# Raw scores and maxima nearer to the scores, their transposition in the raw bank at the beat's end

## The chip, the cores and the metric

The kernel runs on one core of a Trainium2 chip. The metric is the device time in microseconds (us) of one execution, as the median of several runs. The engines are TensorE (PE, with its weight loads shown apart as PEld), VectorE (DVE), ScalarE (ACT), GpSimd (POOL) and SyncE (SP), which only issues DMAs here.

## The reference

One transformer block with conditioning and a second residual, for 32 sequences of 128 tokens with 128 channels:

```
a = x + attention(norm1(x))          # 16 heads of 8 channels, softmax over 128 keys
y = a + swiglu(norm2(a))             # 512 hidden channels
out = x + y
norm(x) = gain(cond) * x * rsqrt(mean(x*x) + eps) + bias(cond)
attention: softmax(q k^T / sqrt(8)) v, then Wo;  swiglu: silu(x Wg) * (x Wh) Wo
```

All of it is in float32. The kernel splits float32 numbers into a high and a low part (or into three bfloat16 parts for queries and keys), so that products of the parts give the accuracy.

## The kernel before

The 32 sequences are cut into G = 8 groups of four. A group's attention takes eight beats, each with half the heads (four heads of either half) of one sequence. The main loop runs over beats T = 0 to 78; in each, every engine does what `due(T, offset, n, every)` says is due: a step with offset o of group g falls into beat 8g + o. All stages of different groups so run side by side in one hand-written order, the same in every beat, and every engine executes its list strictly in that order. Beat T computes the scores of T.

The softmax subtracts the row maximum inside the score product: two rows of the stacked queries hold the negated maximum as a high and a low bfloat16 part. So the maxima must be known before the scores. They are had in these steps:

- `b_raw(g, t)` on PE (L383): eight small products give raw scores into the PSUM buffer `raw` of two banks (in the prologue of group 0 also into `score`). It waits until the maximum of the raw scores before it has been taken.
- `b_max(g, t)` on DVE (L766): a reduction over `raw` gives the negated maxima of that beat, into `nmax`.
- `b_maxT(g, half)` on PE (L393): after four maxima, the half of `nmax` is transposed into the fourth quarter of the bank `pv`.
- `b_shift(g, half)` on DVE (L776, L778): copies it to bfloat16, then subtracts to get the low part.
- `shift_rows(g, half)` on SP (L262): four small DMAs, for each of two sequences one of the high and one of the low part, write the rows into the stacked queries `qs`.
- `c_score(g, t)` on PE (L410) waits for those rows in beats t = 0, 2, 4, 6 of the group.

In the kernel before, raw scores run seven beats ahead of the scores (RAW = -7), and the transpositions lie at offsets -3 and +1 (MAXT = -3, every 4), so in beats 5 and 1 mod 8, one beat after the fourth and eighth maximum. The prologue does the raw scores 0 to 6 of group 0 and the first transposition. `c_pv` of the beat after a transposition waits for the second shift instruction, since it writes the bank that this one reads.

PE's order in a beat: `c_score`, `b_raw`, `c_pv` (L427), `c_tro` (L442, transposition of o_s, odd beats), `d_gate_up` (L320 to L322, the two products into the hidden layer), `b_maxT`, `a_transpose` (L334, odd beats), `d_out` (L489), `c_wo` (L446, odd beats), `d_xt2` (L454, even beats), `c_tr2` (L437, even beats), values, keys and queries of a later group.

DVE's order: `d_final`, `c_x1` (L803, L806, even beats), `d_hi` (L814), the rests of queries and keys (L738), `b_max`, `b_shift`, `d_hidden` (L823 gated, L828 hT), `c_norm` (L786 reciprocal, L791 o_s, even beats), `a_hi` (L730). ScalarE's: `a_high`, the exponential (L607), `c_ot` (L613), the middle part of keys (L600), `c_oT` (L619), `d_tanh` (L636), mean squares (L569), `d_norm` (L625), `a_norm` (L577), the middle part of queries (L600), values (L588).

The gate_up product of a piece goes to the one bank `ffn` and waits for the hT of the piece before, until piece SPREAD; from there on it goes round `raw`'s two banks and `ffn`. SP's order in a beat is store (L268), `shift_rows`, stacking of queries and keys (L254).

Of the kernel before, what the change touches and what calls it, by code (L numbers as in the profile page):

```python
# [15 lines left out]
def bass_cond_transformer_block(  # L16
# [10 lines left out]
    L, B, D = x.shape  # L27
# [5 lines left out]
    G = B // NB  # L33
# [3 lines left out]
    HQ = 4  # L37
# [26 lines left out]
    MEAN, INV1, SCALE1, XT1, HI1 = -30, -28, -26, -23, -15  # L64
    VALUE, KEY, QUERY = -7, -14, -13
    STACK = -12
    RAW, MAXT = -7, -3
    PV = 1
    OT, TR2, NORM, TRO, WO, X1, INV2, XT2, HI2, RESID = 2, 2, 2, 3, 3, 4, 5, 6, 7, 6
    FFN, OUT, FINAL, WSTEP = 10, 15, 17, HC + 1  # L70
    LAST = BEATS * (G - 1) + FINAL + WSTEP
    SPREAD = BEATS * G + RAW + 1 - FFN

    ctx = ExitStack()
    with ctx:
# [146 lines left out]
            return (tok, ffn)[b % 2][:, 0:L] if early(g) else score[:, (b % 2) * 512:(b % 2) * 512 + L]  # L222

        def raw_dst(g, t):
            return score if g == 0 and t % 2 and t < BEATS - 1 else raw

        def key_dst(g):
            return pv if g == 1 else proj
# [88 lines left out]
        def _(pe):  # L317
# [50 lines left out]
            def b_raw(g, t):  # L368
                if t == 0:
                    pe.wait_ge(s_stack[buf(g)], stacked(g))  # L370
                if g == 0:
                    if t == 0:
                        pe.wait_ge(s_xn1, 2 * NB)
                    if t == BEATS - 1:
                        pe.wait_ge(s_max, t)
                    elif t >= 2:
                        pe.wait_ge(s_max, t - 1)
                else:
                    pe.wait_ge(s_max, BEATS * g + t)
                for j in range(HQ):  # L380
                    for e in range(HALVES):
                        h8 = HQ * (t % 2) + j
                        mm = pe.matmul(raw_dst(g, t)[:, pair_cols(e, j)],  # L383
                                       qs[buf(g)][tile_rows(e, RAW_ROWS), h8, batch_cols(t)],
                                       ks[buf(g)][tile_rows(e, RAW_ROWS), h8, batch_cols(t)], start=True, stop=True)
                mm.then_inc(s_raw, 1)

            def b_maxT(g, half):
                pe.wait_ge(s_max, BEATS * g + HQ * (half + 1))
                if g == 0 and half == 0:  # L390
                    pe.wait_ge(s_nmax0, 2)
                    pe.wait_ge(s_krest, 2)
                pe.transpose(pv[:, 3 * L:4 * L], nmax[g % 2][:, half * 128:half * 128 + 128],  # L393
                             ident[:]).then_inc(s_maxT, 1)

            def c_score(g, t):
                if t % 2 == 0:
                    pe.wait_ge(s_shiftrow[buf(g)][t // 2], shifted(g))
                if t == 0 and g < NBUF:
                    pe.wait_ge(s_onerows[g], 32)  # L400
                if g == 0 and t == 0:
                    pe.wait_ge(s_max, BEATS - 2)
                for f, b in due(BEATS * g + t - 1, XT1, NB, 2, since=3):
                    pe.wait_ge(s_xn1, NB * f + b + 1)
                if BEATS * g + t > 0:
                    pe.wait_ge(s_exp, BEATS * g + t)
                for j in range(HQ):
                    for e in range(HALVES):
                        h8 = HQ * (t % 2) + j
                        mm = pe.matmul(score[:, pair_cols(e, j)],  # L410
                                       ks[buf(g)][tile_rows(e, HALF_ROWS), h8, batch_cols(t)],
                                       qs[buf(g)][tile_rows(e, HALF_ROWS), h8, batch_cols(t)], start=True, stop=True)
                mm.then_inc(s_score, 1)

            def c_pv(g, t, T):
# [3 lines left out]

                for f, i in due(T - 1, XT2, NB, 2):  # L420
                    pe.wait_ge(s_xn2, NB * f + i + 1)
                for f, half in due(T - 1, MAXT, 2, HQ):
                    pe.wait_ge(s_slo, 2 * f + half + 1)
                for e in range(HALVES):
                    for j in range(HQ):
                        at = e * HH * VW + (HQ * (t % 2) + j) * VW
# [29 lines left out]
            def d_gate_up(g, p):  # L456
# [6 lines left out]
                if 0 < n < SPREAD:  # L463
                    pe.wait_ge(s_h, n)
                elif SPREAD <= n < SPREAD + 2:
                    pe.wait_ge(s_max, BEATS * G)
                elif n >= SPREAD + 2:
                    pe.wait_ge(s_h, n - 2)
                cs = slice(ch * 128, ch * 128 + 128)
# [51 lines left out]
            unread_products(4)  # L521
            b_raw(0, 4)
            b_maxT(0, 0)
            b_raw(0, 5)
            a_transpose(2, 0)
            a_transpose(2, 1)
            a_values(0)
            a_transpose(2, 2)
            b_raw(0, 6)
            a_transpose(2, 3)  # L530
            for T in range(LAST + 1):
                for g, t in due(T, 0, BEATS):
# [6 lines left out]
                    c_tro(g, i)  # L539
                for g, p in due(T, FFN, PIECES):  # L540
                    d_gate_up(g, p)
                for g, half in due(T, MAXT, 2, HQ):
                    b_maxT(g, half)
                for g, b in due(T, XT1, NB, 2, since=3):
                    a_transpose(g, b, T)
                for w in range(WIN):
# [3 lines left out]
                    c_wo(g, i)  # L550
                for g, i in due(T, XT2, NB, 2):
                    d_xt2(g, i, T)
                for g, i in due(T, TR2, NB, 2):
                    c_tr2(g, i)
                for g, _ in due(T, VALUE, since=1):
# [159 lines left out]
        def _(dve):  # L715
# [54 lines left out]
            def b_shift(g, half):  # L770

                dve.wait_ge(s_maxT, 2 * g + half + 1)
                if g > 0:
                    for b in range(MB):
                        dve.wait_ge(s_shiftrow[buf(g - 1)][MB * half + b], shifted(g - 1))
                dve.tensor_copy(shift[:, half, 0, :], pv[0:MROWS, 3 * L:4 * L]).then_inc(s_shi, 1)  # L776
                dve.wait_ge(s_shi, 2 * g + half + 1)
                dve.tensor_tensor(shift[:, half, 1, :], pv[0:MROWS, 3 * L:4 * L], shift[:, half, 0, :],  # L778
                                  ALU.subtract).then_inc(s_slo, 1)

            def c_norm(g, i):
# [83 lines left out]
            for t in range(HQ):  # L865
                b_max(0, t)
            b_shift(0, 0)
            for t in range(HQ, BEATS - 1):
                b_max(0, t)
            for T in range(LAST + 1):  # L870
                for g, w in due(T, FINAL, WIN, WSTEP):
                    d_final(g, w)
# [187 lines left out]
```

## Time and profile before

| | us |
|---|---|
| median of 3 runs | 257.99 |
| lowest, highest | 257.29, 258.37 |
| the profiled execution's own time | 255.85 |
| its span | 254.0 |
| first score, last exponential (start) | 32.39, 230.65 |

The share of the span in which each engine was busy, the busy time by tenths in 40 slices of 6.35 us, and the clock granted to TensorE:

```profile
span 254.0 us, 8307 instructions
...
PE   3496677779989999999989999999999999899894
PEld 2384454457668868786878877877787878687893
DVE  4648866888898989889888998899888997564673
ACT  5355748867865786569756776667757655666430
POOL 8324852695283345526282526152623232324310
PEclk9999979999999999999999999999999999999999
```

A digit 9 is 90% or more of a slice. The steady loop fills the slices from about the tenth to the thirty-fourth. A matmul's end is modelled, so that a busy PE is not PE at its peak. Times in the text without a unit are places in the trace, in us from the start of the span.

### The profile page before, as it was taken

The page shows a single profiled execution, that of the slowest core. Times are in us where ns is not written, and L with a number is a line of the kernel's source. Part 1 is how long each engine was busy: PE and PEld are TensorE (multiplying, and loading weights), DVE is VectorE, ACT ScalarE, POOL GpSimd, SP SyncE. Part 2 cuts the span into 40 slices and gives each one's busy share as a digit, 9 for nine tenths or more (in the row PEclk, how much of TensorE's full clock was granted, in tenths as well). Part 3 has the DMA queues.
Part 4 walks back from the last instruction along what each step waited for, and adds up shares of the span by engine and source line. Part 5 has one row for each costly group of instructions (what it writes and reads, how often), then busy time and mean ns, then how long its engine had stood idle before and what let it go on. Part 6 is the DMA issues. An engine that isn't in the chain of part 4 may idle for free.

```text
span 254.0 us, 8307 instructions
## 1 busy us (share of the span) xinstructions
PE 223.3 (88%) x3084; PEld 180.8 (71%) x3084; DVE 203.0 (80%) x490; ACT 163.4 (64%) x352; POOL 112.0 (44%) x183
## 2 busy tenths in 40 slices
PE   3496677779989999999989999999999999899894
PEld 2384454457668868786878877877787878687893
DVE  4648866888898989889888998899888997564673
ACT  5355748867865786569756776667757655666430
POOL 8324852695283345526282526152623232324310
PEclk9999979999999999999999999999999999999999
DMA  5867602510360026001530054004500000000001
GB/s 166 343 169 169 169 4 65 156 45 5 85 170 1 27 66 186 26 24 40 156 85 18 11 151 122 4 26 128 147 3 26 1 26 3 23 3 25 22 23 41
DMA packets 18819, 18.79 MB, mean 74 GB/s; under 512 B 3644, under 2 KB 17980, under 8 KB 18652
## 3 DMA queue, kind: packets, MB, share of 16 engines
q1 hardware_dynamic: 18252, 17.80, 24.9%
q10 hardware_dynamic: 528, 0.46, 0.8%
q8 instruction: 25, 0.41, 0.7%
q14 instruction: 14, 0.11, 0.2%
HBM read 3.22 MB, written 2.10 MB: 21 GB/s over the span
## 4 chain that ended last, share of the span: by engine, by line
PE 43%; issue 24%; POOL 16%; DVE 6%; ACT 4%; SPq 3%; ACTq 1%; DMA 1%; POOLq 0%; DVEq 0%
PE proj L489 7%; PE pv L427 6%; PE ffn L320 5%; PE score L410 4%; PE ffn L322 3%; PE ffn L321 3%; SPq L254 3%; POOL inv L933 3%; PE raw L383 2%; POOL qp L925 2%; PE tok L442 2%; POOL xn_lo L946 2%; POOL kp L925 2%; POOL xs L939 2%; POOL xn_lo L918 2%
## 5 line engine op out<-in xcount | busy, mean ns | idle before, releaser
L766 DVE TENSOR_REDUCE nmax<-raw 128x8 f32<-128x1024 f32 x61 | 74.2, 1217 | 2.8 <-PE raw L383 2.6
L607 ACT ACTIVATE p_s<-score 128x1024 f32<-128x1024 f32 x64 | 65.4, 1022 | 17.1 <-PE score L410 15.9
L427 PE MATMUL pv<-p_s,va 128*32 128x128 f32 x1024 | 41.7, 280 | 1.9 <-ACT xn L625 1.2
L320 PE MATMUL ffn<-xn_hi,ffn_hi 128*128 128x256 f32 x106 | 34.8, 328 | 1.2 <-POOL xn_lo L946 1.2
L636 ACT ACTIVATE th<-ffn 128x256 f32<-128x256 f32 x53 | 20.4, 384 | 19.6 <-PE ffn L322 19.6
L489 PE MATMUL proj<-ffn_out_s,hT 128*128 128x128 f32 x240 | 31.6, 275 | 0.0
L823 DVE SCALAR_TENSOR_TENSOR gated<-th,ffn 128x256 f32<-128x256 f32 x53 | 22.0, 415 | 12.0 <-ACT th L636 11.7
L427 PEld LDWEIGHTS pv<-p_s,va 128*32 128x32 f32 x1024 | 24.7, 109 | 9.3 <-issue 4.1
L946 POOL TENSOR_TENSOR xn_lo<-xn,xn_hi 128x128 fp32r<-128x128 f32 x32 | 14.7, 460 | 34.6 <-DVE xn_hi L814 34.6
L322 PE MATMUL ffn<-xn_hi,ffn_lo 128*128 128x256 f32 x106 | 29.7, 280 | 0.0
L321 PE MATMUL ffn<-xn_lo,ffn_hi 128*128 128x256 f32 x106 | 29.6, 279 | 0.0
L489 PEld LDWEIGHTS proj<-ffn_out_s,hT 128*128 128x128 f32 x240 | 29.2, 191 | 0.0
L410 PE MATMUL score<-qs,ks 64*128 64x128 bf16 x512 | 25.6, 220 | 2.6 <-ACT p_s L607 0.9
L933 POOL TENSOR_TENSOR inv<-ms,mhalf 128x1 f32<-128x1 f32 x32 | 17.4, 544 | 21.5 <-DVE ms L806 21.5
L320 PEld LDWEIGHTS ffn<-xn_hi,ffn_hi 128*128 128x128 f32 x106 | 21.4, 202 | 6.5 <-issue 4.2
L383 PE MATMUL raw<-ks,qs 62*128 62x128 bf16 x488 | 24.0, 217 | 1.4 <-DMA qs<-qp 0.9
L410 PEld LDWEIGHTS score<-qs,ks 64*128 64x128 bf16 x512 | 14.6, 94 | 14.6 <-issue 9.7
L828 DVE SCALAR_TENSOR_TENSOR hT<-gated,ffn 128x256 f32<-128x256 f32 x53 | 22.3, 421 | 1.8
L625 ACT ACTIVATE xn<-pv,mod 128x128 f32<-128x128 f32 x32 | 14.5, 454 | 10.0 <-PE pv L454 9.1
L321 PEld LDWEIGHTS ffn<-xn_lo,ffn_hi 128*128 128x128 f32 x106 | 20.1, 189 | 0.0
L322 PEld LDWEIGHTS ffn<-xn_hi,ffn_lo 128*128 128x128 f32 x106 | 19.9, 188 | 0.0
L925 POOL TENSOR_TENSOR qp<-q_rest,qp 128x512 bf16<-128x512 f32 x7 | 8.7, 1240 | 23.3 <-ACT qp L600 23.3
(132 smaller groups left out, 469.2 us busy)
## 6 DMA issues: line engine op xcount, KB each, us to landing
ks<-kp SPq DMA_DIRECT2D x48, 128.0 KB, 2.4
qs<-qp SPq DMA_DIRECT2D x45, 128.0 KB, 2.5
out_y<-x_s SPq DMA_DIRECT2D x16, 128.0 KB, 1.8
x_s<-in_x SPq DMA_DIRECT2D x1, 1536.0 KB, 10.0
qs<-shift SPq DMA_DIRECT2D x64, 4.0 KB
x_s<-in_x SPq DMA_DIRECT2D x2, 256.0 KB, 3.5
ffn_in_s<-in_ffn_in_w SPq DMA_DIRECT2D x1, 512.0 KB, 6.7
qs<-qp ACTq DMA_DIRECT2D x3, 128.0 KB, 3.7
```

The lines of the kernel that those rows point to most:

```text
L320: pe.matmul(dst, w_hi, v_hi, start=True, stop=False)
L321: pe.matmul(dst, w_hi, v_lo, start=False, stop=False)
L322: return pe.matmul(dst, w_lo, v_hi, start=False, stop=True)
L383: mm = pe.matmul(raw_dst(g, t)[:, pair_cols(e, j)], qs[buf(g)][tile_rows(e, RAW_ROWS), h8, batch_cols(t)], ks[buf(g)][tile_rows(e, RAW_ROW ...
L410: mm = pe.matmul(score[:, pair_cols(e, j)], ks[buf(g)][tile_rows(e, HALF_ROWS), h8, batch_cols(t)], qs[buf(g)][tile_rows(e, HALF_ROWS), h8 ...
L427: mm = pe.matmul(pv[VW * j:VW * j + VW, (t % 2) * L:(t % 2 + 1) * L], va[vbuf(g)][:, t // 2, at:at + VW], p_s[:, (BEATS * g + t) % PBUF, p ...
L489: mm = pe.matmul(out_dst(g, w)[:, b * D:(b + 1) * D], hT[:, HC * w + ch, b * L:(b + 1) * L], ffn_out_s[:, ch, :], start=(ch == 0 and b == ...
L607: act.activation(p_s[:, n % PBUF, :], score[:], ACT.Exp, scale=SCALE).then_inc(s_exp, 1)
L766: dve.tensor_reduce(heads[:, :, t % 2, :], raw_dst(g, t)[:].rearrange("l (e j m) -> l e j m", e=HALVES, j=HQ), AX.X, ALU.max, negate=True) ...
L823: dve.scalar_tensor_tensor(out=gated[:], in0=th[:, p % 2, :], scalar=1.0, in1=ffn_dst(n)[:, 0:PW], op0=ALU.add, op1=ALU.mult).then_inc(s_g ...
L828: dve.scalar_tensor_tensor(out=hT[:, p, :], in0=gated[:], scalar=0.5, in1=ffn_dst(n)[:, PW:2 * PW], op0=ALU.mult, op1=ALU.mult).then_inc(s ...
L933: pool.tensor_tensor(inv2[:, i:i + 1], ms2[:, i:i + 1], mhalf[:, 0:1], ALU.pow).then_inc(s_inv2, 1)
```

## The change

The raw scores and maxima run five beats ahead of the scores (RAW = -5), the transpositions lie at offsets -2 and +2 (beats 6 and 2 mod 8), in the beat of the fourth and eighth maximum itself. PE does them at the end of the beat, after `d_xt2` and before `c_tr2`, and they write the first quarter bank of `raw` (only the very first one still `pv`). The raw scores after a transposition (t = 0 and 4) wait for the second shift instruction; `c_pv` no longer does, except in the first beat. The prologue has two raw scores and two maxima fewer. DVE's, ScalarE's and SP's lists within a beat stay as they are. SPREAD goes from 48 to 53: pieces 48 to 52 stay on the one bank.

```diff
--- before.py
+++ after.py
@@ -64,12 +64,12 @@
     MEAN, INV1, SCALE1, XT1, HI1 = -30, -28, -26, -23, -15
     VALUE, KEY, QUERY = -7, -14, -13
     STACK = -12
-    RAW, MAXT = -7, -3
+    RAW, MAXT = -5, -2
     PV = 1
     OT, TR2, NORM, TRO, WO, X1, INV2, XT2, HI2, RESID = 2, 2, 2, 3, 3, 4, 5, 6, 7, 6
     FFN, OUT, FINAL, WSTEP = 10, 15, 17, HC + 1
     LAST = BEATS * (G - 1) + FINAL + WSTEP
-    SPREAD = BEATS * G + RAW + 1 - FFN
+    SPREAD = BEATS * G + MAXT + 1 - FFN
 
     ctx = ExitStack()
     with ctx:
@@ -222,7 +222,10 @@
             return (tok, ffn)[b % 2][:, 0:L] if early(g) else score[:, (b % 2) * 512:(b % 2) * 512 + L]
 
         def raw_dst(g, t):
-            return score if g == 0 and t % 2 and t < BEATS - 1 else raw
+            return score if g == 0 and t in (1, 3) else raw
+
+        def maxT_dst(g, half):
+            return pv[:, 3 * L:4 * L] if g == 0 and half == 0 else raw[:, 0:L]
 
         def key_dst(g):
             return pv if g == 1 else proj
@@ -371,12 +374,14 @@
                 if g == 0:
                     if t == 0:
                         pe.wait_ge(s_xn1, 2 * NB)
-                    if t == BEATS - 1:
+                    if t >= HQ + 1:
                         pe.wait_ge(s_max, t)
                     elif t >= 2:
                         pe.wait_ge(s_max, t - 1)
                 else:
                     pe.wait_ge(s_max, BEATS * g + t)
+                    if t % HQ == 0:
+                        pe.wait_ge(s_slo, 2 * g + t // HQ)
                 for j in range(HQ):
                     for e in range(HALVES):
                         h8 = HQ * (t % 2) + j
@@ -390,7 +395,7 @@
                 if g == 0 and half == 0:
                     pe.wait_ge(s_nmax0, 2)
                     pe.wait_ge(s_krest, 2)
-                pe.transpose(pv[:, 3 * L:4 * L], nmax[g % 2][:, half * 128:half * 128 + 128],
+                pe.transpose(maxT_dst(g, half), nmax[g % 2][:, half * 128:half * 128 + 128],
                              ident[:]).then_inc(s_maxT, 1)
 
             def c_score(g, t):
@@ -399,7 +404,7 @@
                 if t == 0 and g < NBUF:
                     pe.wait_ge(s_onerows[g], 32)
                 if g == 0 and t == 0:
-                    pe.wait_ge(s_max, BEATS - 2)
+                    pe.wait_ge(s_max, HQ)
                 for f, b in due(BEATS * g + t - 1, XT1, NB, 2, since=3):
                     pe.wait_ge(s_xn1, NB * f + b + 1)
                 if BEATS * g + t > 0:
@@ -419,8 +424,8 @@
 
                 for f, i in due(T - 1, XT2, NB, 2):
                     pe.wait_ge(s_xn2, NB * f + i + 1)
-                for f, half in due(T - 1, MAXT, 2, HQ):
-                    pe.wait_ge(s_slo, 2 * f + half + 1)
+                if g == 0 and t == 0:
+                    pe.wait_ge(s_slo, 1)
                 for e in range(HALVES):
                     for j in range(HQ):
                         at = e * HH * VW + (HQ * (t % 2) + j) * VW
@@ -463,7 +468,7 @@
                 if 0 < n < SPREAD:
                     pe.wait_ge(s_h, n)
                 elif SPREAD <= n < SPREAD + 2:
-                    pe.wait_ge(s_max, BEATS * G)
+                    pe.wait_ge(s_slo, 2 * G)
                 elif n >= SPREAD + 2:
                     pe.wait_ge(s_h, n - 2)
                 cs = slice(ch * 128, ch * 128 + 128)
@@ -521,12 +526,10 @@
             unread_products(4)
             b_raw(0, 4)
             b_maxT(0, 0)
-            b_raw(0, 5)
             a_transpose(2, 0)
             a_transpose(2, 1)
             a_values(0)
             a_transpose(2, 2)
-            b_raw(0, 6)
             a_transpose(2, 3)
             for T in range(LAST + 1):
                 for g, t in due(T, 0, BEATS):
@@ -539,8 +542,6 @@
                     c_tro(g, i)
                 for g, p in due(T, FFN, PIECES):
                     d_gate_up(g, p)
-                for g, half in due(T, MAXT, 2, HQ):
-                    b_maxT(g, half)
                 for g, b in due(T, XT1, NB, 2, since=3):
                     a_transpose(g, b, T)
                 for w in range(WIN):
@@ -550,6 +551,8 @@
                     c_wo(g, i)
                 for g, i in due(T, XT2, NB, 2):
                     d_xt2(g, i, T)
+                for g, half in due(T, MAXT, 2, HQ):
+                    b_maxT(g, half)
                 for g, i in due(T, TR2, NB, 2):
                     c_tr2(g, i)
                 for g, _ in due(T, VALUE, since=1):
@@ -773,9 +776,9 @@
                 if g > 0:
                     for b in range(MB):
                         dve.wait_ge(s_shiftrow[buf(g - 1)][MB * half + b], shifted(g - 1))
-                dve.tensor_copy(shift[:, half, 0, :], pv[0:MROWS, 3 * L:4 * L]).then_inc(s_shi, 1)
+                dve.tensor_copy(shift[:, half, 0, :], maxT_dst(g, half)[0:MROWS, :]).then_inc(s_shi, 1)
                 dve.wait_ge(s_shi, 2 * g + half + 1)
-                dve.tensor_tensor(shift[:, half, 1, :], pv[0:MROWS, 3 * L:4 * L], shift[:, half, 0, :],
+                dve.tensor_tensor(shift[:, half, 1, :], maxT_dst(g, half)[0:MROWS, :], shift[:, half, 0, :],
                                   ALU.subtract).then_inc(s_slo, 1)
 
             def c_norm(g, i):
@@ -865,8 +868,7 @@
             for t in range(HQ):
                 b_max(0, t)
             b_shift(0, 0)
-            for t in range(HQ, BEATS - 1):
-                b_max(0, t)
+            b_max(0, HQ)
             for T in range(LAST + 1):
                 for g, w in due(T, FINAL, WIN, WSTEP):
                     d_final(g, w)
```

## Rows read from the trace of the kernel before

**Rows 1.** Part 1 of the page: busy time, share of the span and instructions of each engine.
```profile
PE 223.3 (88%) x3084; PEld 180.8 (71%) x3084; DVE 203.0 (80%) x490; ACT 163.4 (64%) x352; POOL 112.0 (44%) x183
```

**Rows 2.** Busy time by stretch; each line lists busy us and instructions per engine, then clock.
```profile
130.42:156.63 26.21, 25.79 (x382) 21.23 (x382) 23.75 (x58) 18.49 (x38) 11.71 (x21) 1.00 0.27 74
150.84:154.27 3.43, 3.43 (x52) 3.00 (x52) 2.97 (x9) 2.67 (x6) 2.41 (x4) 1.00 0.76 202
...
156.63:160.44 3.81, 3.46 (x51) 2.93 (x51) 3.23 (x8) 2.47 (x6) 0.78 (x2) 1.00 0.11 35
```

**Rows 3.** The waits view: who waited for whom; total us, times, longest.
```profile
PEld tok L442 <- DVE o_s L791: 7.4, 13, 1.1
...
DVE shift L776 <- PE pv L393: 3.3, 8, 1.1
```

**Rows 4.** Timeline of beat 37: start, length, engine, line, operation, in brackets idle before it.
```profile
152.84 0.27 PE L393 MATMUL pv<-ident,nmax 128*128 128x128 f32 x1
...
153.04 0.38 ACT L636 ACTIVATE th<-ffn 128x256 f32<-128x256 f32 x1 [0.26 <-PE ffn L322]
...
153.15 0.28 DVE L776 CAST shift<-pv 32x128 bf16<-32x128 f32 x1 [0.36 <-PE pv L393]
...
153.67 0.40 DVE L823 SCALAR_TENSOR_TENSOR gated<-th,ffn 128x256 f32<-128x256 f32 x1
```

**Rows 5.** Timeline of beats 38 and 39.
```profile
155.31 1.22 DVE L766 TENSOR_REDUCE nmax<-raw 128x8 f32<-128x1024 f32 x1
...
156.21 0.27 PE L454 MATMUL pv<-ident,xs 128*128 128x128 f32 x1
...
156.41 0.38 ACT L636 ACTIVATE th<-ffn 128x256 f32<-128x256 f32 x1 [0.40 <-PE ffn L322]
...
156.82 0.42 DVE L823 SCALAR_TENSOR_TENSOR gated<-th,ffn 128x256 f32<-128x256 f32 x1 [0.29 <-ACT th L636]
...
158.25 0.33 PE L442 MATMUL tok<-ident,o_s 128*128 128x128 f32 x1 [0.32 <-DVE o_s L791]
```

**Rows 6.** Timeline of beats 34 and 35.
```profile
142.26 1.21 DVE L766 TENSOR_REDUCE nmax<-raw 128x8 f32<-128x1024 f32 x1
...
142.95 0.30 PE L454 MATMUL pv<-ident,xs 128*128 128x128 f32 x1
...
143.46 0.42 DVE L823 SCALAR_TENSOR_TENSOR gated<-th,ffn 128x256 f32<-128x256 f32 x1
...
145.62 0.63 ACT L600 ACTIVATE kp<-k_rest 128x512 bf16<-128x512 f32 x1
...
146.13 0.28 ACT L619 ACTIVATE oT_s<-tok 128x128 f32<-128x128 f32 x1
...
146.47 0.49 PE L446 MATMUL tok<-attn_w_s,oT_s 128*128 128x128 f32 x2
```

**Rows 7.** Timeline of beats 27 and 51, the instructions of PE that waited.
```profile
117.77 0.64 PE L427 MATMUL pv<-p_s,va 128*32 128x128 f32 x16 [0.34 <-ACT xn L625]
...
196.91 0.33 PE L442 MATMUL tok<-ident,o_s 128*128 128x128 f32 x1 [0.27 <-DVE o_s L791]
```

**Rows 8.** Timeline of the end of the prologue.
```profile
28.38 0.28 DVE L778 TENSOR_TENSOR shift<-pv,shift 32x128 bf16<-32x128 f32 x1
...
32.39 0.40 PE L410 MATMUL score<-qs,ks 64*128 64x128 bf16 x8 [0.89 <-DMA qs<-shift]
```

**Rows 9.** The chain of waits that ended last: start, length, what.
```profile
30.13 0.56 SPq L262
```

**Rows 10.** Timeline of beats 58 and 59.
```profile
218.16 0.08 DVE L806 DVE_READ_ACCUMULATOR2_ANT ms<- 128x1 f32 x1
...
219.07 0.42 DVE L823 SCALAR_TENSOR_TENSOR gated<-th,raw 128x256 f32<-128x256 f32 x1 [0.83 <-ACT th L636]
...
220.50 0.33 PE L442 MATMUL tok<-ident,o_s 128*128 128x128 f32 x1 [0.32 <-DVE o_s L791]
```

**Rows 11.** Busy time by stretch, beat 1; columns as in rows 2.
```profile
33.90:37.70 3.80, 3.79 (x42) 2.96 (x42) 2.57 (x6) 1.48 (x2) 0.94 (x4) 0.58 0.00 0
```

## Prediction

> **What bounds the kernel now.** The page comes first: by its first part PE is busy 88% of the span, DVE 80%, the weight load 71% [rows 1]. Next, the busy time by stretch shows why no single share decides. In a steady stretch of eight beats (scores 30 to 38, 26.21 us) PE is busy 25.79 us and DVE 23.75; beat 37 alone has PE busy 3.43 of 3.43 us [rows 2]. So PE runs nearly without a hole, with DVE close behind it, and a wait put into PE's queue is lost unless PE would have waited soon anyway. The waits view shows where it does: the longest DVE wait of PE in the loop is that of tok L442 (the transposition of o_s, `c_tro`) for DVE's o_s, 7.4 us in 13 times [rows 3]. The chain behind that wait is gate_up, tanh, gated, hT, reciprocal, o_s, transposition, and it goes through DVE's queue in program order. I therefore read the timeline beat by beat. I name beats by the number T of their score, and "6 mod 8" says where in a group's eight beats one lies. The question for each moved instruction is what stands behind it.
>
> **Part 1: the transposition of the maxima goes from beats 5 and 1 (mod 8) to the end of beats 6 and 2, where the last maximum it needs is taken in the same beat.** It costs PE the same issue slot, 0.11 us (the next PE instruction starts that much after 152.84 [rows 4]); one beat loses it, the next has it. What changes is the order of waits. DVE's program is unchanged inside a beat: `b_max`, `b_shift`, `d_hidden`, `c_norm`. In beat 37 the shift pair cost DVE little, as its maximum was old: gated started at 153.67, while tanh had ended at 153.42 (153.04 + 0.38) [rows 4]. Without the pair gated starts there at 153.45, and DVE, which has no idle time after it, reaches the maximum of beat 38 0.22 us sooner: it ends at 156.31 and not 156.53 (155.31 + 1.22 [rows 5]).
>
> Beat 38 afterwards: PE has its last instruction before the transposition, xt2, at 156.21, now 0.11 earlier (0.11 issue slot gone from beat 37), so it is free at about 156.21; the maximum ends at 156.31, and 0.06 later the transposition starts (156.37). DVE's copy starts 0.31 after a transposition starts (152.84 to 153.15 [rows 4]): 156.68. The pair holds DVE for 0.52 (153.15 to 153.67), so gated starts at 157.20 where it now starts at 156.82 [rows 5]: 0.38 later. Everything behind it on DVE follows in a row: hT, reciprocal, o_s, and PE's transposition at 158.25 was already waiting for o_s by 0.32 us [rows 5]. So that delay goes straight into PE: **0.38 us for such a beat pair**. The new wait of the next raw product for the second shift instruction ends at about 157.3, some 0.45 after the raw product of before; it and the pv product behind it are done by 158.4, so it hides behind the wait for o_s; its own cost is 0, and 0.45 if that cover is gone. Beats 14, 22 and 30 start their gate_up late for another reason (POOL), so the 0.11 of PE buys nothing but DVE is likewise late; I take 0.32. Sum for the six beats 14 to 54: 3 x 0.32 + 3 x 0.38 = **2.1 us**.
>
> Beat 34 (2 mod 8), same steps: the maximum ended at 142.26 + 1.21 = 143.47, afterwards 143.25. PE's xt2 is at 142.95, afterwards 142.84 [rows 6]. PE stands until 143.31 for the maximum, which makes the rest of its beat, with the key product, 0.3 us late. On DVE gated, now at 143.46, starts at 143.31 + 0.31 + 0.52 = 144.14, 0.68 late. Behind it on DVE, without a hole, is k_rest, then ScalarE's kp from k_rest (145.62), and behind that in ScalarE's queue oT (146.13), for whose end (146.41) PE's L446 at 146.47 waits [rows 6]: oT then ends near 147.1, and PE loses 0.6 to 0.7 us in all. I take 0.7 for beats 34 and 42. In beats 10, 18 and 26 ScalarE has mean squares to do, and PE's pv of the next beat already waits 0.34 us for ScalarE's xn (117.77) [rows 7]; this hides most, and I take 0.15 each. Beat 50 has no key product, so PE does not stand, but its L442 at 196.91 has already waited 0.27 for o_s [rows 7], and gated comes late by the steps above; 0.3. Sum: 2 x 0.7 + 3 x 0.15 + 0.3 = **2.1 us**.
>
> **Part 2: raw scores and maxima two beats later.** Two raw products and two maxima leave the prologue. They were not on the path: the first score starts at 32.39 after a wait of 0.89 us for the DMA of the shift rows, whose data were ready at 28.66 (28.38 + 0.28) but which SP issues only at 30.13, behind group 1's stacking [rows 8, 9]. SP's order there is untouched. So the gain is 0. The beats 0 and 1 have a raw product each as before. The early beats have no gate_up; the transposition in beats 2 and 6 holds DVE's normalisation by some 0.1 to 0.2 us, and beat 1 loses a transposition at the half clock: **0.2 us** together. The stacking has two beats more until raw products need it; it was not waited for in the loop, so 0.
>
> At the other end beats 57 and 58 get raw products, maxima and, in beat 58, the last shift pair. DVE has room in beat 57, but now in beat 58 gated (219.07) stands behind x1, a maximum of 1.22 and the shift pair. By the steps above: the square of x1 is done at 218.24 (218.16 + 0.08), the maximum then ends at 219.46, and 0.06 + 0.31 + 0.52 later, at about 220.3, gated starts, 1.2 us late; PE's L442 at 220.50 has waited 0.32 us for o_s [rows 10], so it is 1.2 late too. Then five more gate_up products (48 to 52) run on one bank instead of three; the beat is longer than the loop gate_up, tanh, hT there, save once by some 0.2. **1.4 us.**
>
> **Part 3: other waits.** pv no longer waits for the shift, a wait that the rows read above never show; 0. A batch's rows are two small DMAs. In the prologue the first was issued at 30.13 [rows 9] and the score that waits for both started at 32.39 [rows 8], so at most 2.3 us go from first issue to last landing. Issued at about 157.0, the rows of the first batch are there at 159.3; the score that reads them starts at 160.44 (the end of beat 39 [rows 2], afterwards later still): 1.1 us of slack, price 0. SP's queue: the store of the same beat comes before them, the stacking before that is done by then, as SP issued the shift of beat 37 already in that beat; in beats 2 to 4 the shift's issues can push stacking DMAs back by about a microsecond, with more than five beats until they are needed.
>
> **Sum.** 2.1 + 2.1 + 0.2 + 1.4 = 5.8 us. The profiled execution took 255.85 us (span 254.0); that makes 261.7. It lies 2.1 us under the median of the three runs, 257.99, so I add the sum to the median: **263.8 us**, 2.2% slower. Unknown sizes: the part of a delay that PE's later waits take back, from none to half of the steady terms (-2 to +1), the tail (0.7 to 2), and the clock. The granted clock was 0.58 from 33.90 to 37.70, that is at the level of 1.2 GHz for most of it [rows 11], after PE had waited in the prologue. The prologue loses PE work, so the half-clock stretch can come earlier, where PE waits anyway, or last longer; the stretch cost at most 3.79 x 0.42 = 1.6 us, so this is -1.6 to +1.6, and I take 0. Own range of the forecast: 260.8 to 267.
>
> **Rivals.**
> (a) *The delays are absorbed.* DVE's total work is unchanged, so if throughput and not the order of waits rules, only the tail counts: 258.0 + 0 to 1.4, about **258.8**. For it: DVE's 23.75 of 26.21. Against: the gaps of PE at L442 are of order, not of load. Trace Analysis of the Trainium skill (Identifying the Most-Contended Engine) says to go by occupancy, and by the weight load rather than matmul time for TensorE. That makes DVE, 80% against 71%, the engine to watch, and since the change leaves its work alone the time would not move; the trace agrees that DVE is highly loaded and does not bear out that it alone sets the beat.
> (b) *Faster: the odd beats gain.* If beats 1 and 5 mod 8 are set by DVE, losing the shift pair there saves 0.22 us in each of 13 and the even beats hide it behind tanh, whose wait before gated was 0.29 us in beat 38 [rows 5]: 13 x 0.22 = 2.9, less the tail's 1.4: **256.5**. It decides only where the maximum ends over 0.9 us before tanh does, so that the transposition, copy and second copy fit. In beat 38 tanh ends at 156.79, 0.26 after the maximum. Against it also PE's 3.43 of 3.43.
> (c) *The rows land late.* If in the loop the landing takes 1.1 us more than in the prologue, the scores 0 and 4 of each group wait; each further 0.3 us costs 15 x 0.3 = 4.5: **268**. For it: one beat and not two is left for the way. Against: 1.1 us of slack.
>
> **Chances.** Forecast 0.73, (a) 0.12, (b) 0.08, (c) 0.07. A measurement of this kernel can tell about 0.5% (1.3 us) from no change. Faster by more than that: (b) and a clock gain in (a), 0.09. Within: most of (a), 0.11. Slower: 0.80. The range 258.6 to 267.2 leaves out (b), part of (a) and (c).
>
> **What would show it.** DVE's copy of the maxima (L776 of before) should have idle time before it in nearly all 16 cases, near 0.4 us each and not 8 cases with 3.3 in all [rows 3]; PE's transposition should wait for the maximum in beats 2 mod 8; PE's waits at `c_tro` for o_s should grow by 3 us or more; beats 7 mod 8 should take about 4.1 and not 3.8 us; the first score should stay at 32.4; DVE's and PE's busy sums should not move. The forecast is wrong if beats 7 and 3 keep their lengths, or if scores 0 or 4 show a DMA wait.

## The result, and the profile after

The changed kernel takes 261.89 us (median of 5 runs, 260.60 to 262.93), the kernel before 258.37 (5 runs, 257.29 to 258.57). The ratio on record is 1.0171, 95% interval 1.0136 to 1.0207: slower, by 1.4 to 2.1%. Measured again beside a later set of kernels (after_again below) the ratio on record is 1.0171 too (1.0138 to 1.0205). A ratio on record is not the quotient of the two medians, which is 1.0136 the first time and 1.0181 (261.30 against 256.66) the second. It leaves out executions over 1.5% slower than the fastest of their kernel, which below concerns old_even alone: two of its four, the profiled one among them. Forecast was 263.8 us, plus 5.8; the medians differ by 3.5 us the first time and by 4.6 the second, the two profiled executions by 4.75.

The page of the changed kernel, its first two parts (as [rows 1]) and one group of the fifth part:

```profile
span 258.7 us, 8299 instructions
...
PE 226.0 (87%) x3084; PEld 181.6 (70%) x3084; DVE 202.2 (78%) x490; ACT 164.2 (63%) x352; POOL 111.9 (43%) x183
...
PEclk9996599999999999999999999999999999999999
...
L388 PE MATMUL raw<-ks,qs 62*128 62x128 bf16 x496 | 24.9, 220 | 2.3 <-DVE shift L781 1.8
```

DVE has no more work than before (202.2 against 203.0 us), yet the span is 4.75 us longer. The raw product (L388) has a wait that was not there: for the second shift instruction, 1.8 us in all. Lines moved by a few: L398 is the transposition of the maxima, L779 and L781 the shift pair, L447 `c_tro`, L451 `c_wo`, L826 gated.

The busy time by stretch says where the 4.75 us arose. First beats 10 to 57, then 57 to 63, of the kernel before:

```profile
59.73:214.08 154.35, 148.04 (x2201) 121.08 (x2201) 137.27 (x331) 107.27 (x230) 66.69 (x112) 1.00 0.23 63
214.08:230.21 16.13, 15.14 (x218) 12.05 (x217) 8.85 (x34) 11.18 (x22) 5.43 (x11) 1.00 0.06 18
```

and of the changed kernel:

```profile
58.38:217.35 158.97, 150.00 (x2202) 121.12 (x2202) 136.84 (x331) 108.20 (x230) 66.16 (x111) 1.00 0.23 61
217.35:234.91 17.56, 15.70 (x232) 12.39 (x233) 11.12 (x36) 11.29 (x22) 5.43 (x11) 1.00 0.06 18
```

The steady part lost 4.62 us, with the same instructions on every engine but for a record or two (DVE x331 in both) and the clock at its full level. The tail lost 1.43. Up to beat 10 the changed kernel was 1.34 us ahead. 4.62 + 1.43 - 1.34 and 0.04 at the very end make 4.75. Of the 1.34 us, 0.74 had come before the first score, which starts at 31.65 and not at 32.39; the section on the prediction says why.

The timeline of beats 38 and 39 of the changed kernel, which answers to [rows 5]:

```profile
155.74 1.22 DVE L769 TENSOR_REDUCE nmax<-raw 128x8 f32<-128x1024 f32 x1
...
156.72 0.27 PE L459 MATMUL pv<-ident,xs 128*128 128x128 f32 x1
...
156.92 0.38 ACT L639 ACTIVATE th<-ffn 128x256 f32<-128x256 f32 x1 [0.40 <-PE ffn L325]
...
157.02 0.33 PE L398 MATMUL raw<-ident,nmax 128*128 128x128 f32 x1
...
157.38 0.28 DVE L779 CAST shift<-raw 32x128 bf16<-32x128 f32 x1 [0.42 <-PE raw L398]
...
157.90 0.40 DVE L826 SCALAR_TENSOR_TENSOR gated<-th,ffn 128x256 f32<-128x256 f32 x1
...
158.12 0.40 PE L388 MATMUL raw<-ks,qs 62*128 62x128 bf16 x8 [0.23 <-DVE shift L781]
...
159.31 0.33 PE L447 MATMUL tok<-ident,o_s 128*128 128x128 f32 x1 [0.21 <-DVE o_s L794]
```

Read it from the top. The maximum ends at 156.96, the transposition starts 0.06 later, DVE's copy 0.36 after that, and gated 0.52 behind the copy. tanh had ended at 157.30, so gated is 0.6 us late. In beat 38 PE itself stands from about 156.83 (the 0.11 us slot after xt2 at 156.72) to 157.02. Counted from the score of beat 38 (154.79, before 154.27), gated now starts at +3.11 and not at +2.55, and the transposition of o_s at +4.52 and not +3.98.

Beats 34 and 35, which answer to [rows 6], on ScalarE and PE:

```profile
143.24 0.33 PE L398 MATMUL raw<-ident,nmax 128*128 128x128 f32 x1 [0.20 <-DVE nmax L769]
...
144.13 0.40 DVE L826 SCALAR_TENSOR_TENSOR gated<-th,ffn 128x256 f32<-128x256 f32 x1
...
146.25 0.63 ACT L603 ACTIVATE kp<-k_rest 128x512 bf16<-128x512 f32 x1 [0.20 <-DVE k_rest L741]
...
146.78 0.26 ACT L622 ACTIVATE oT_s<-tok 128x128 f32<-128x128 f32 x1
...
147.09 0.49 PE L451 MATMUL tok<-attn_w_s,oT_s 128*128 128x128 f32 x2 [0.40 <-ACT oT_s L622]
```

This is the predicted chain, k_rest to kp to oT to PE, with PE's wait for oT at its end. Counted from the score of beat 34 (140.71, before 140.91) L451 starts at +6.38 and not +5.56.

### The profile page after: what moved, and what is told of

The parts are those of the page before. It is cut to its first block, busy times and chain, and to the rows that moved or that the text cites. A ratio compares the mean times of both kernels' runs of the same rounds, so it can differ in the third digit from the quotient of the medians.

```text
span 258.7 us, 8299 instructions
## 1 busy us (share of the span) xinstructions
PE 226.0 (87%) x3084; PEld 181.6 (70%) x3084; DVE 202.2 (78%) x490; ACT 164.2 (63%) x352; POOL 111.9 (43%) x183
## 4 chain that ended last, share of the span: by engine, by line
issue 39%; PE 26%; POOL 20%; DVE 7%; ACT 2%; SPq 2%; DMA 2%; POOLq 0%; DVEq 0%; ACTq 0%
PE proj L494 4%; POOL inv L935 4%; POOL xn_lo L948 3%; PE pv L432 3%; POOL xs L941 3%; PE ffn L323 3%; POOL kp L927 2%; POOL qp L927 2%; PE raw L388 2%; SPq L257 2%; POOL resid L956 2%; PE ffn L325 2%; PE ffn L324 2%; PE score L415 2%; DMA qs<-qp 2%
## 5 line engine op out<-in xcount | busy, mean ns | idle before, releaser
L769 DVE TENSOR_REDUCE nmax<-raw 128x8 f32<-128x1024 f32 x62 | 75.5, 1218 | 4.0 <-PE raw L388 4.0
L323 PE MATMUL ffn<-xn_hi,ffn_hi 128*128 128x256 f32 x112 | 36.5, 326 | 2.0 <-POOL xn_lo L948 1.6
L826 DVE SCALAR_TENSOR_TENSOR gated<-th,ffn 128x256 f32<-128x256 f32 x56 | 23.3, 415 | 17.4 <-ACT th L639 17.0
L639 ACT ACTIVATE th<-ffn 128x256 f32<-128x256 f32 x56 | 21.5, 384 | 20.4 <-PE ffn L325 20.4
L325 PE MATMUL ffn<-xn_hi,ffn_lo 128*128 128x256 f32 x112 | 31.4, 280 | 0.0
L324 PE MATMUL ffn<-xn_lo,ffn_hi 128*128 128x256 f32 x112 | 31.3, 279 | 0.0
L323 PEld LDWEIGHTS ffn<-xn_hi,ffn_hi 128*128 128x128 f32 x112 | 22.6, 201 | 7.8 <-issue 4.5
L388 PE MATMUL raw<-ks,qs 62*128 62x128 bf16 x496 | 24.9, 220 | 2.3 <-DVE shift L781 1.8
L831 DVE SCALAR_TENSOR_TENSOR hT<-gated,ffn 128x256 f32<-128x256 f32 x56 | 23.6, 421 | 1.9
L324 PEld LDWEIGHTS ffn<-xn_lo,ffn_hi 128*128 128x128 f32 x112 | 21.2, 189 | 0.0
L325 PEld LDWEIGHTS ffn<-xn_hi,ffn_lo 128*128 128x128 f32 x112 | 21.0, 188 | 0.0
L388 PEld LDWEIGHTS raw<-ks,qs 62*128 62x128 bf16 x496 | 16.7, 96 | 4.7 <-issue 3.2
```

The costliest lines, as they stand in the source:

```text
L323: pe.matmul(dst, w_hi, v_hi, start=True, stop=False)
L324: pe.matmul(dst, w_hi, v_lo, start=False, stop=False)
L325: return pe.matmul(dst, w_lo, v_hi, start=False, stop=True)
L388: mm = pe.matmul(raw_dst(g, t)[:, pair_cols(e, j)], qs[buf(g)][tile_rows(e, RAW_ROWS), h8, batch_cols(t)], ks[buf(g)][tile_rows(e, RAW_ROW ...
L769: dve.tensor_reduce(heads[:, :, t % 2, :], raw_dst(g, t)[:].rearrange("l (e j m) -> l e j m", e=HALVES, j=HQ), AX.X, ALU.max, negate=True) ...
L826: dve.scalar_tensor_tensor(out=gated[:], in0=th[:, p % 2, :], scalar=1.0, in1=ffn_dst(n)[:, 0:PW], op0=ALU.add, op1=ALU.mult).then_inc(s_g ...
```

## Experiments

A kernel's stretches below are the differences between the starts of its scores 0, 10, 16, 57 and 63 in its trace. Beats 10 to 16 (19.7 to 23.0 us) are left out, because in late_rows a half-clock stretch reaches just into them.

| kernel | median us | ratio to before (95%) | 0-10 | 16-57 | 57-63 |
|---|---|---|---|---|---|
| before | 258.37 | | 27.33 | 134.45 | 16.13 |
| changed | 261.89 | 1.0171 (1.0136-1.0207) | 26.74 | 138.71 | 17.56 |
| old_even | 263.32 | 1.0154 (1.0083-1.0225) | 31.62 | 138.31 | 16.50 |
| shift_behind | 264.78 | 1.0303 (1.0235-1.0371) | 28.32 | 140.79 | 17.03 |
| after_dup | 265.59 | 1.0345 (1.0312-1.0378) | 28.27 | 140.95 | 17.77 |
| before_dup | 256.50 | 0.9989 (0.9968-1.0009) | 28.22 | 134.86 | 16.32 |
| late_rows | 289.91 (1 run) | | 38.14 | 151.41 | 20.11 |
| spread53 | 256.80 | 0.9992 (0.9970-1.0015) | 28.28 | 134.47 | 16.64 |
| warm | 255.01 | 0.9924 (0.9899-0.9949) | 26.28 | 134.53 | 16.12 |
| norm_first | 255.45 | 0.9937 (0.9912-0.9962) | 27.53 | 133.75 | 16.12 |
| after_again | 261.30 | 1.0171 (1.0138-1.0205) | 26.74 | 138.69 | 17.56 |
| after_warm | 262.19 | 1.0225 (1.0185-1.0265) | 26.43 | 138.68 | 17.56 |
| warm_norm_first | 253.89 | 0.9888 (0.9863-0.9912) | 26.26 | 133.79 | 16.13 |
| warm_norm_first_2_6 | 253.29 | 0.9880 (0.9846-0.9915) | 26.23 | 133.85 | 15.75 |

The kernel before, measured again beside the experiments, had medians of 256.66 to 256.99 us. The ratios are the numbers to compare. The stretches are those of one profiled execution each, in which the half-clock stretch near the start can lie elsewhere than in the others.

**The transposition moved alone: old_even.** From the kernel before:

```diff
-    RAW, MAXT = -7, -3
+    RAW, MAXT = -7, -2
...
                     c_tr2(g, i)
+                for g, half in due(T, MAXT, 2, HQ):
+                    b_maxT(g, half)
```

The destination is `tok[:, 2 * L:3 * L]`, the old place behind `d_gate_up` is empty, and `c_pv` no longer waits for the shift, except in the first beat. The new place is one step later than in the change, behind `c_tr2`.

> The kernel before with raw scores still seven beats ahead, but the transpositions at the end of the beats 6 and 2 mod 8 (after c_tr2, into the third quarter of the bank tok), so with a maximum that is two beats old: nothing waits for a maximum of the same beat, and no raw product waits for the shift. Theory 'place': the shift pair stands on DVE ahead of gated, hT and o_s and can start only when PE has come to the end of its beat, so beats 6 and 7 mod 8 lose nearly what they lose in the changed kernel (gated about 0.4 us late after the transposition), in all +2 to +3.5 us against before (ratio 1.008 to 1.014). Theory 'same beat': what costs is that PE and DVE wait for the maximum of the same beat; then this kernel is within 0.5 us of before (ratio 1.00). Rival 'load': as before too.

Measured 1.0154, from two of its four runs, so that the interval is wide (1.0083 to 1.0225); the four lie between 259.38 and 265.41, and the profiled one (264.78) has a second half-clock stretch, in beats 8 and 9. The reading therefore rests on beats 16 to 57, where the clock is at its full level. They take 138.31 us: the kernel loses 3.9 there, of the changed kernel's 4.3, and somewhat more than the 2 to 3.5 expected. Its raw scores are where they were and no transposition waits for a maximum of its own beat. Three lines of its timeline, beat 38:

```profile
162.54 0.38 ACT L639 ACTIVATE th<-ffn 128x256 f32<-128x256 f32 x1 [0.40 <-PE ffn L325]
...
162.98 0.28 DVE L779 CAST shift<-tok 32x128 bf16<-32x128 f32 x1 [0.40 <-PE tok L396]
...
163.50 0.40 DVE L826 SCALAR_TENSOR_TENSOR gated<-th,ffn 128x256 f32<-128x256 f32 x1
```

DVE idles 0.40 us for PE to come to the transposition, then does the pair, and gated is 0.58 behind tanh (162.54 + 0.38 = 162.92). So the place (end of PE's beat, ahead of gated on DVE) is enough for nearly the whole steady loss. The same-beat wait and the place are two bounds that end at nearly the same time, and taking away one leaves the other. The loss is laid out differently: beats 38 and 39 grow by 0.11 and 0.41 us here, by 0.35 and 0.19 in the changed kernel.

**The order on DVE: shift_behind.** From the changed kernel, `b_shift` comes after `d_hidden`:

```diff
-                for g, half in due(T, MAXT, 2, HQ):
-                    b_shift(g, half)
...
                 for g, p in due(T, FFN, PIECES):
                     d_hidden(g, p)
+                for g, half in due(T, MAXT, 2, HQ):
+                    b_shift(g, half)
```

> The changed kernel, with DVE's shift pair behind gated and hT instead of ahead of them. Theory 'chain' as in the prediction (the delay of gated, hT and o_s is the cost, the raw product's wait for the second shift is covered): o_s comes no later than now, but the raw product waits for a shift that ends some 0.6 us later, and pv, which stands behind it, ends about 0.35 us after the present time of c_tro, so the cover is gone and this kernel is slower than the changed one by 2 to 4 us, ratio to before 1.025 to 1.033. If the place of gated alone were the cost, the loss of the changed kernel would be gone: ratio 1.00 to 1.005. Rival 'load' (only DVE's total counts): ratio 1.017, as the changed kernel.

Measured 1.0303. The waits view shows what took over from the wait for o_s:

```profile
PE raw L388 <- DVE shift L781: 8.1, 9, 1.2
...
PEld tok L447 <- DVE o_s L794: 3.1, 5, 1.1
```

The pair's place on DVE matters to two customers on PE: what hangs on gated, and the raw product of the next beat, with pv and everything else behind it. Either order makes one of them wait: here the raw product (8.1 us in 9 waits), in the changed kernel mostly what hangs on gated (7.8 us of waiting for o_s in 16). It is not the worse order in every beat. Beats 19, 27, 35 and 43 (3 mod 8) are 0.2 to 0.3 us shorter here than in the changed kernel; beats 15, 23, 31, 39, 47 and 55 are 0.3 to 0.7 us longer, and beat 51 0.6. Moving the pair behind gated in beats 18, 26, 34 and 42 alone was not tried.

**More of the same work: after_dup and before_dup.** In both, one more copy of the maxima:

```diff
+                dve.tensor_copy(spare[:], <the same source>)
                 dve.tensor_copy(shift[:, half, 0, :], <the source>).then_inc(s_shi, 1)
```

> The changed kernel, with the first shift instruction done twice (once into a spare tile): 0.28 us more DVE work in 16 beats, 4.5 us in all. Theory 'chain': in the beats 6 and 2 mod 8 it goes straight into gated, o_s and PE's c_tro, so 0.2 to 0.28 us in some 13 beats: 2.5 to 3.6 us over the changed kernel's 261.9, ratio to before 1.024 to 1.031. Rival 'load': the same as in the kernel before with the same doubling, whatever that is; if DVE has room, nothing: ratio 1.017.

> The kernel before with the same doubling, there in beats 5 and 1 mod 8. Theory 'chain': the beats 5 and 1 are set by PE, and gated of the beat behind them waits 0.3 us for tanh anyway, so at most 0.5 us: ratio 1.000 to 1.002. Rival 'load': if the total of DVE sets the pace, 2.5 to 4.5 us as in the changed kernel, ratio 1.010 to 1.017.

This decides against the rival of load. With the same extra instruction the ratio rises by 1.7% in the changed kernel (1.0345 against 1.0171, more than forecast) and not at all in the kernel before (0.9989). In beats 16 to 57, with ten shift pairs, it costs 2.24 us (0.22 each, 140.95 - 138.71) against 0.41. Beats 10 to 63 together take 2.6 us more than in the changed kernel, 1.0%, and that is within what was forecast. The rest of the profiled execution's excess over the changed kernel's, 1.5 us, lies in beats 0 to 10, where the half-clock stretch fell (30.8 to 37.6), and is not shown to be the copy's. DVE in beat 38 of after_dup:

```profile
160.65 0.28 DVE L780 CAST spare<-raw 32x128 bf16<-32x128 f32 x1 [0.42 <-PE raw L399]
160.86 0.27 DVE L781 CAST shift<-raw 32x128 bf16<-32x128 f32 x1
...
161.37 0.40 DVE L828 SCALAR_TENSOR_TENSOR gated<-th,ffn 128x256 f32<-128x256 f32 x1
```

**Rows that land too late: late_rows.** The transposition one beat after the maximum, in the old place (MAXT = -1 with RAW = -5, bank pv).

> Raw scores five beats ahead as in the changed kernel, but the transposition one beat after the maximum (beats 7 and 3 mod 8), in the old place behind gate_up and in the bank pv. No wait for a maximum of the same beat, no shift pair ahead of c_norm. Theory: no loss from DVE's order, but the shift rows are ready about 3.4 us later than before and only 1 us before the score that reads them; first issue to landing takes 2.3 us, so the scores 0 and 4 of each group wait for the DMA, 1.3 to 1.5 us for score 0 and up to 2.5 us for score 4, where SP is still issuing stacking DMAs: together 20 to 30 us, 276 to 288 us. If the landing is much quicker in the loop, 257 to 262 us.

```profile
PEld score L410 <- DMA qs<-shift: 27.9, 16, 2.5
```

289.91 us, one run, just above the forecast. Sixteen times PE waited for the rows before a score, 1.7 us on average. The granted clock was at half from 32.3 to 39.2 and again from 46.0 to 69.9, which is in the 38.14 us of beats 0 to 10. So with raw scores five beats ahead, of the two places tried one is late for gated and the other late for the rows. In the changed kernel only the weight load of the very first score waited for rows, 0.4 us.

**The tail: spread53.** The kernel before with `SPREAD = BEATS * G + RAW + 6 - FFN`.

> The kernel before with SPREAD at 53: the hidden-layer products 48 to 52 stay on one bank, as in the changed kernel; nothing else. Theory: the tail's loss (beats 57 to 63 take 1.43 us more in the changed kernel's profile, 17.56 against 16.13) is the shift pair and the maximum of beat 58, and this part is worth 0 to 0.3 us (ratio 1.000 to 1.001). Rival: the one bank is what costs in the tail, 1 us or more there (ratio 1.004).

In the trace beats 57 to 63 take 16.64 us, 0.51 more than before; the median shows nothing (0.9992, and its interval leaves room for 0.4 us). Of the 0.51, 0.33 lie in beat 60 and 0.18 in beat 58. Beat 60 is 0.33 longer in the changed kernel and in after_dup too (0.18 in shift_behind), and unchanged in old_even and before_dup, which keep the old SPREAD: that part is the one bank. The rest of the changed kernel's 1.43 us lies in beats 58 and 59 (0.95 and 0.19). There the timeline of the changed kernel, which answers to [rows 10], shows the forecast chain:

```profile
222.57 0.33 PE L398 MATMUL raw<-ident,nmax 128*128 128x128 f32 x1 [0.53 <-DVE nmax L769]
...
223.46 0.40 DVE L826 SCALAR_TENSOR_TENSOR gated<-th,ffn 128x256 f32<-128x256 f32 x1
...
224.86 0.33 PE L447 MATMUL tok<-ident,o_s 128*128 128x128 f32 x1 [0.84 <-DVE o_s L794]
```

Counted from the score of beat 58 (219.66, before 216.44) gated starts at +3.80 and not +2.63, the transposition of o_s at +5.20 and not +4.06. How much of the 0.18 of the one bank in beat 58 hides in this is not shown.

**The start: warm and after_warm.** Six unread products where PE waits for the first rows:

```diff
             a_transpose(2, 3)
+            pe.wait_ge(s_va, 1)
+            unread_products(6)
```

> The kernel before with six more unread products of PE at the end of the prologue, where PE waits for the DMA of the first shift rows. If the half-clock stretch of 3 to 7 us around beats 0 and 1 comes from PE's idle time just before it, beats 1 and 2 take up to 1.5 us less: ratio 0.994 to 0.998. If it comes from what lies further back (in the changed kernel's profile it began at 21.2, before any instruction that differs), nothing: ratio 1.00.

> The changed kernel with six more unread products of PE at the end of the prologue. Theory 'clock': the same 1.5 to 2 us as in the kernel before (there 0.9924), so 0.992 times the changed kernel's ratio, about 1.010 to 1.015; the loss of the change itself stays, since it lies in the beats. Against it would be a ratio like that of the changed kernel without them.

In the kernel before they give 0.8% (interval 0.5 to 1.0%). The granted clock over the whole execution is 0.993 to 0.998 in five of warm's six, while its median in the 23 executions of the kernel before beside it is 0.986. The changed kernel does not gain (1.0225 against 1.0171, with intervals that overlap), so this forecast fell. The stretch views of the two profiled executions show part of the reason. After_again, whose beats 10 to 57 and 57 to 63 came out as expected (158.95 and 17.56 us), and its ratio too for a stretch that lies ahead of beat 0:

```profile
24.00:28.00 4.00, 4.00 (x28) 2.98 (x27) 3.68 (x4) 1.89 (x14) 3.75 (x7) 0.50 0.76 205
28.00:32.40 4.40, 4.26 (x38) 3.44 (x37) 1.97 (x5) 4.06 (x9) 3.90 (x5) 0.57 0.49 130
32.40:40.00 7.60, 5.34 (x99) 4.00 (x100) 5.03 (x9) 5.95 (x16) 3.56 (x6) 1.00 0.00 1
```

and of after_warm:

```profile
24.00:28.00 4.00, 2.82 (x33) 1.88 (x33) 3.64 (x4) 1.85 (x13) 3.75 (x7) 1.00 0.77 205
28.00:32.40 4.40, 3.16 (x23) 2.34 (x24) 1.69 (x3) 4.02 (x9) 3.90 (x5) 1.00 0.47 129
```

Without the extra products the changed kernel had its 1.2 GHz stretch in the prologue, where PE has work for only 3.16 of 4.40 us at the full clock, the extra products included. Without the stretch beats 0 to 10 take 0.31 us less (26.43 against 26.74), but the six products themselves, which start at 31.38 and take 0.97 us, put the first score at 32.29 and not 31.67. Nothing is left of the gain. The kernel before has the stretch, in its profile, in beat 1 [rows 11]. In the other three executions of after_warm the granted clock was 0.980 to 0.987, no higher than in after_again's (0.977 to 0.987), so there the products did not raise it; these were not profiled.

**Faster than both: norm_first and its sequels.** The theory says that in beats 7 mod 8 PE waits for the o_s that DVE makes in beats 6 mod 8 behind gated and hT. So they change places there (the kernel before, otherwise untouched):

```diff
+                if T % BEATS == 6:
+                    for g, i in due(T, NORM, NB, 2):
+                        c_norm(g, i)
                 for g, p in due(T, FFN, PIECES):
                     d_hidden(g, p)
...
+                if T % BEATS != 6:
```

> The kernel before with DVE's normalisation (reciprocal, o_s) ahead of gated and hT in beats 6 mod 8 alone. Theory 'chain': PE's c_tro of beats 7 mod 8, which waits for o_s (0.3 to 0.6 us there), comes as soon as pv ends, about 0.35 us sooner, but gate_up behind it waits for hT, 0.5 us later than now, so that 0.1 us of it stays: six beats, -0.3 to -1 us (ratio 0.996 to 0.999). Rival 'load': nothing, 1.00.

> The kernel before with both edits that were faster alone (0.9924 and 0.9937). They act in different stretches, so the gains should add: ratio 0.984 to 0.989.

> The same, with the normalisation ahead of gated and hT in beats 2 mod 8 as well. There tanh and the transposition for the normalisation end at nearly the same time, and PE's c_tro of beat 35 did not wait for o_s, while k_rest and hT stand behind; theory 'chain': no more than 0.3 us of gain in beats 50 and 58, none elsewhere: within 0.2% of the kernel with beats 6 alone.

norm_first gave 0.9937, more than the 0.996 to 0.999 expected; its interval (0.9912 to 0.9962) just reaches it. Beat 39 takes 3.65 us where it took 3.81, and the profiled execution gains 0.84 us from beat 10 to 57; what the medians show beyond that is not explained. The wait for o_s is down from 7.4 us [rows 3] to the first line, and the next bound, hT before gate_up, appears in the second (0.3 us, once, in the kernel before):

```profile
PEld tok L442 <- DVE o_s L791: 3.3, 6, 1.1
...
PEld ffn L320 <- DVE hT L828: 1.2, 7, 0.3
```

With both edits (warm_norm_first) the ratio is 0.9888 (0.9863 to 0.9912), 1.1% faster than the kernel before: less than the product of the two gains (0.986), within what was expected. The third step makes no difference that the ratio can tell, as forecast; in its profile beat 59 is 0.39 us shorter.

## Why the prediction was right, point by point

- **Direction and mechanism: right.** The steady terms were 2.1 + 2.1 = 4.2 us; measured 4.62. From the starts of the scores: the six pairs from beat 14 to 55, each taken with the beat before it as in the forecast, grew by 0.36, 0.33, 0.33, 0.44, 0.54 and 0.57 us (forecast 0.32 and 0.38), in sum 2.6 and not 2.1. Beats 34 and 42 with their neighbours cost 0.7 and 0.8 (forecast 0.7), beats 18 and 26 0.1 each and beat 10 nothing (0.15 each), beat 50 0.3 (0.3).
- **The cover of the raw product's wait: partly wrong.** The step priced the wait for the second shift instruction at 0, hidden behind the wait for o_s. It hides in part. The o_s wait should have grown by 3 us or more; in the waits view it went from 7.4 to 7.8 us. The loss sits in the waits in front of it, which PE meets first, here by PE's own rows of that view: for the maximum (2.2 us in 6 waits), for the shift (1.8 in 8) and, in beats 3 mod 8, for oT (2.7, before 1.3). The beats' lengths were nevertheless near: 4.01 us for beat 39 against a forecast of about 4.1, because the other part of the loss, 0.35 us, fell into beat 38.
- **The transposition itself was undersized**: the next PE instruction starts 0.16 us after it when PE has just stood (157.02 to 157.18), not 0.11, and the copy starts 0.36 and not 0.31 after it. Together that is about the 0.1 us per pair missing above.
- **The tail: right**, 1.43 against 1.4 us: 1.14 in beats 58 and 59, where 1.2 was forecast, and 0.33 in beat 60 for the one bank, where 0.2 was.
- **The term that failed was the start.** The prediction put +0.2 us there, with the first score at 32.4, and took the clock as unchanged, with -1.6 to +1.6 as its bounds. Measured was -1.34, in two parts. The first score came at 31.65, 0.74 us sooner, because SP issued the rows at 29.38 and not at 30.13 [rows 9]. The three stacking issues ahead of them took 1.91 us, in the kernel before 2.68, one of them 1.38. Whether the change did that is open. Such a long issue (0.5 to 1.1 us above the others) stands in the profiles of all eight kernels with the old prologue, and four of the six with the shorter one are without it; but shift_behind, with the changed kernel's prologue, has one, issued the rows at 30.47 and started its first score at 32.74. The other 0.60 us lie in beats 0 to 10, and there in the clock: in the changed kernel's profile the half-clock stretch ran from 21.2 to 31.5 us, so it ended before the first score, while in that of before it covered beat 1, which alone is 1.05 us shorter now. The stretch began before the first instruction that differs, so its place there is not shown to be due to the change. It lay in the same place in both profiles of the changed kernel, but at 33.4 to 40.2 in shift_behind and 30.8 to 37.6 in after_dup, whose prologue is the same but for one copy on DVE in the second.
- **The signs named beforehand.** DVE's copy of the maxima idles in all 16 cases, 8.3 us together, as said, and PE's transposition waits for the maximum. The growth of the o_s wait and the first score at 32.4 did not come. DVE's busy sum hardly moved (203.0 to 202.2); PE's went from 223.3 to 226.0 with as many instructions. The wait of pv for the shift, priced at 0, was in the kernel before 0.2 us, once.
- **The absolute number** was built on a median of 257.99 from three runs; with five it was 258.37. Without the start the profiles differ by 6.1 us (4.62 + 1.43 + 0.04) where 5.6 was forecast; with it by 4.75 where 5.8 was. The forecast holds either way, but the total is smaller than the sum only by the start, which the forecast's mechanism has no part in.
- **Rival (a), load**, is excluded by the doubled copy. **Rival (b)** is excluded by the beats 5 mod 8: from beat 21 on they gained 0.10 to 0.12 us each, the slot of the transposition and nothing of DVE's 0.22. **Rival (c)** did not occur, and late_rows shows what it would have cost.

## What to carry to other kernels

When two engines take turns in a beat, price a moved instruction by what stands behind it on its engine and where the partner's queue reaches the instruction that releases it, not by its length: the same 0.28 us copy cost 0.22 us in one beat and 0.04 in the beat before. When a wait is removed, look for the second bound that ends at the same time. A look-ahead that is shortened costs time if what stands behind it (here the transposition, the shift and at most 2.3 us from the first issue of the rows to their last landing) then has to fit into too few beats.

## What the runs showed of the hardware that was not expected

The place of TensorE's half-clock stretch near the start differs between kernels whose programs are the same up to there: 21.2 to 31.5 us (changed), 25.0 to 28.4 (warm), 33.7 to 37.1 (before), 32.9 to 39.7 (before_dup), none (after_warm). It also differs between executions of one kernel, by the granted clock of the whole: 0.967 to 0.993 in 23 executions of the kernel before. Beats 0 to 10 take 26.2 to 26.4 us where none of it falls there (warm, after_warm, warm_norm_first), and 28.2 to 28.3 where 6.8 us of it do (before_dup, spread53). A microsecond of unread products ahead of the first score was worth 0.8% in one kernel and nothing in the other. What sets the place of the stretch stays open. So does why one issue of SP in the prologue, 0.6 us long as a rule, took 1.4 us in the kernel before, 1.7 in warm and 1.2 in old_even.
